# Cross-attention block with a quantised MLP: a split wait on TensorE, another form for five VectorE copies, and one step moved in VectorE's order

## The reference, cut to what matters

```python
# B=32 batches, T=100 tokens, D=256, S=361 context rows, H=16 heads of DK=64
Qh = einsum('btd,hdk->bhtk', layernorm(x), WQ)
Kh = einsum('btd,hdk->bhtk', ctx, WK)
Vh = einsum('btd,hdv->bhtv', ctx, WV)
attn = softmax(Qh @ Kh.T / sqrt(dk) + mask * -1e9)
x = x + concat_heads(attn @ Vh) @ WO
x = x + qlinear(gelu(qlinear(layernorm(x), W1, b1)), W2, b2)   # 8-bit codes, scales over the whole tensor
```

## Time and profile before

| what | value |
|---|---|
| median of 3 runs | 1129.66 us (1129.05 to 1130.61) |
| the profiled execution | 1126.18 us |
| its span, first to last instruction | 1124.1 us |
| TensorE busy | 1018.1 us, 91% of the span |
| VectorE busy | 978.2 us, 87% |
| ScalarE busy | 865.1 us, 77% |
| GpSimd busy | 770.6 us, 69% |
| the VectorE copies of L946 | 160, 131.5 us in all |

### The profile page before, as it was taken

How to read it: one execution, slowest core, us unless ns; L and a number is a source line. 1 busy time by engine, 2 the same in 40 slices (tenths; PEclk the granted TensorE clock), 3 DMA queues, 4 the chain that set the end, 5 groups by cost and what they waited for, 6 DMA issues and landing times.

```text
span 1124.1 us, 37431 instructions
## 1 busy us (share of the span) xinstructions
PE 1018.1 (91%) x10489; PEld 643.3 (57%) x10489; DVE 978.2 (87%) x2528; ACT 865.1 (77%) x1805; POOL 770.6 (69%) x1108
## 2 busy tenths in 40 slices
PE   3999999999999999999999999999999999985808
PEld 2555566666666666666666666666666666653307
DVE  5777999999999999999999999999999999973997
ACT  4555888888888888888888888888888888873916
POOL 2246877777777777777777777777777777773700
PEclk9999999999999999999999999999999999996969
DMA  8301665555555555555555555555555555555003
GB/s 253 113 1 31 130 134 131 131 135 135 135 135 131 130 135 132 130 131 134 135 135 135 135 135 135 132 130 130 134 135 135 132 130 130 134 132 153 1 0 117
DMA packets 441419, 138.22 MB, mean 123 GB/s; under 512 B 413650, under 2 KB 440374, under 8 KB 441398
## 3 DMA queue, kind: packets, MB, share of 16 engines
q1 hardware_dynamic: 441398, 137.96, 51.0%
HBM read 28.60 MB, written 6.55 MB: 31 GB/s over the span
## 4 chain that ended last, share of the span: by engine, by line
PE 75%; DVE 10%; ACT 5%; issue 4%; POOL 3%; DMA 1%; DVEq 1%; ACTq 0%; SPq 0%; POOLq 0%
PE front L341 19%; PE front L343 17%; PE front L342 17%; PE back L1226 8%; PE front L1208 6%; PE tp L1208 5%; POOL hl L585 3%; DVE hrange L1059 2%; DVE hrange L1060 2%; DVE prob L939 2%; ACT prob L711 2%; DVE k_l L959 1%; ACT q_h L749 1%; PE front L1291 1%; ACT ctx_h L745 1%
## 5 line engine op out<-in xcount | busy, mean ns | idle before, releaser
L585 POOL TENSOR_TENSOR hl<-prob,hl 100x361 f16<-100x361 f32 x512 | 432.1, 853 | 97.2 <-DVE hl L946 50.9
L711 ACT ACTIVATE prob<-prob,nmax 100x361 f32<-100x361 f32 x512 | 293.9, 587 | 47.7 <-DVE nmax L939 47.5
L341 PE MATMUL front<-ctx_h,wk_h 128*128 128x362 f16 x512 | 164.2, 321 | 31.3 <-POOL ctx_l L574 17.8
L1226 PEld LDWEIGHTS back<-v,pT 128*128 128x128 f16 (+1 forms) x4608 | 165.1, 98 | 45.1 <-issue 9.6
L717 ACT ACTIVATE hl<-prob 100x361 f16<-100x361 f32 x352 | 176.0, 500 | 7.9
L1226 PE MATMUL back<-v,pT 128*128 128x65 f16 (+1 forms) x4608 | 174.2, 194 | 6.3 <-DMA pT<-hl 6.2
L343 PE MATMUL front<-ctx_h,wk_l 128*128 128x362 f16 x512 | 161.7, 316 | 0.0
L342 PE MATMUL front<-ctx_l,wk_h 128*128 128x362 f16 x512 | 161.5, 315 | 0.0
L721 ACT ACTIVATE k_h<-front 128x362 f16<-128x362 f32 x256 | 118.9, 464 | 54.7 <-PE front L343 54.7
L959 DVE SCALAR_TENSOR_TENSOR k_l<-front,k_h 128x362 f16<-128x362 f32 x256 | 135.2, 528 | 24.4 <-ACT k_h L721 21.8
L939 DVE CUSTOM_DVE_ANT_0 prob<-front,mask_g,ngain 100x361 f32<-100x361 f32 x256 | 149.6, 584 | 2.2
(11 more groups left out here) (180 smaller groups left out, 1980.8 us busy)
## 6 DMA issues: line engine op xcount, KB each, us to landing
ctx_raw<-ctxT SPq DMA_DIRECT2D x33, 361.0 KB, 3.1
pT<-hl SPq DMA_TRANSPOSE x256, 3.1
xs<-x SPq DMA_DIRECT2D x8, 400.0 KB
q_all<-x SPq DMA_DIRECT2D x32, 100.0 KB
out<-q_all SPq DMA_DIRECT2D x32, 100.0 KB
xb<-out SPq DMA_DIRECT2D x5, 640.0 KB, 7.5
out<-xb SPq DMA_DIRECT2D x25, 128.0 KB, 1.8
q_all<-wq SPq DMA_DIRECT2D x1, 1024.0 KB, 6.6
```

The lines of the kernel that those rows point to most:

```text
L341: eng.matmul(dst, lh, rh, start=first, stop=False)
L585: pool.tensor_tensor(hl[0:T, n % RT, 1, 0:S], prob[0:T, n % RP, 0:S], hl[0:T, n % RT, 0, 0:S], ALU.subtract).then_inc(s_lo, 1)
L711: act.activation(prob[0:T, n % RP, 0:S], prob[0:T, n % RP, 0:S], ACT.Exp, bias=nmax[0:T, n:n + 1], scale=-1.0).then_inc(s_exp, 1)
L1226: ins = pe.matmul(obank[j % 2][:, n % GH * DV:(n % GH + 1) * DV], pT[0:r, n % RT, part_ * ST + st, :], v2[half][0:r, st, v, n % HT, :], st ...
```

## The change

Three edits. The wait of K0 for both pieces of `ctx_l` becomes a wait for the first piece ahead of the first three matmuls and for the second ahead of the other three. The five VectorE copies of a high half of the probabilities in each turn become a multiply by one and add of zero that also writes out a sum, into a new tile `hsum` that nothing reads. The due time of MAX14 becomes 10.619 in place of 9.245, which moves it from the last place of a turn to the place behind K0's low half, that is, `k_l` of K0 goes ahead of MAX14.

```diff
     MAX=(-2.253, -1.786, -0.98, -0.598, 0.248, 0.373, 0.602, 1.062, 3.199, 3.682, 5.123, 7.009, 7.8, 8.323,
-        9.245, 12.252),
+        10.619, 12.252),
...
+    hsum = place("hsum", [P, 1], F32)
...
                     wait(dve, s_exp, H * a + h + 1)
                     wait(dve, s_pv, H * a + h // 2 * 2 + 1 - RT)
-                    dve.tensor_copy(hl[0:T, h % RT, 0, 0:S], prob[0:T, h % RP, 0:S]).then_inc(s_hv, 1)
+                    dve.tensor_scalar(hl[0:T, h % RT, 0, 0:S], prob[0:T, h % RP, 0:S], 1.0, 0.0, ALU.mult, ALU.add,
+                                      accum_out=hsum[0:T, 0:1]).then_inc(s_hv, 1)
...
                 if kind == "K":
-                    if n == 0:
-                        wait(pe, s_c, KD * (a + 1))
                     ms = slice(n * P, (n + 1) * P)
                     for k in range(KD):
+                        if n == 0:
+                            wait(pe, s_c, KD * a + k + 1)
                         ins = split3(pe, ps[:, 0:SE], (wk_h[:, k, ms], wk_l[:, k, ms]),
```

## The result

The changed kernel takes 1121.7 us in the median of 5 runs, against 1129.66 us for the kernel before; the ratio is 0.9934, 95% interval 0.9921 to 0.9947. It is faster by 8.0 us. The forecast was 14.0 us: the direction came out, and so did the wait that sets the turn (K3's, for K1's `k_l`). The size did not, since one step on VectorE was far slower than forecast.

A forecast was written before the change was run, and what follows sets the result against it. TensorE's late starts at a turn's beginning, waiting for `ctx_l` and `k_l`, bound the kernel. They fall from 1.46 to 1.00 us, gaining 0.45 in each of 31 turns, 14.0 us: 1115.7 us forecast, range 1108.5 to 1124.

The forecast's parts named there:

- What bounds the kernel: At a turn's start TensorE waits for `ctx_l` (17.8 us in all) and VectorE's `k_l` (12.3 us); K3's start sets the gain.
- the anchor: TensorE's 521.00, when both `ctx_l` pieces are ready; set by a chain from the last V product that no edit shortens.
- Edit 1: On TensorE, K0's issue ends 0.46 us earlier a turn, with a 0.23 us wait for the second `ctx_l` piece.
- Edit 2: On VectorE, the pass takes 0.52 us and its read 0.08, mostly hidden; head 11's copy ends at 521.6, not 522.89.
- rival 2: GpSimd also holds the copies' new form on VectorE: K3 0.08 us later a turn, 1132.2 us; chance 0.07.
- The failing step: On VectorE at a turn's start, LN4 takes 0.07 us start to start behind head 11's copy, freeing VectorE near 521.7.
- Edit 3: VectorE idles from 521.7 to 522.43 before K0's `k_l`; K2 starts 0.96 us earlier, K3 0.45 us earlier.
- rival 3: Late `k_h` lengthens VectorE's idle time, or a dearer copy takes 0.2 us: gain 0.1 to 0.3 a turn, 1120 to 1126.5; chance 0.11.
- Past K3 all is covered: Later in the turn VectorE is at least as far ahead as TensorE; work queued behind MAX14 comes 0.3 to 0.6 us earlier.
- The signs named beforehand: Passes near 0.52 us, K3 waiting some 0.6, VectorE idling about 0.7; TensorE's `k_l` waits about 20 us, `ctx_l` under 8.

The follow-up runs named there:

- the extra subtraction: Changed kernel plus one unused 361-column GpSimd subtraction, behind LO10 (1113.35 us) or, in a second kernel, ahead of it (1113.77 us).
- The kernels bound at V1: Changed kernel with NORM1 moved behind K1's low half, 1116.25 us; the same without the step LN4, 1110.71 us.

## Why the prediction was right in direction and off in size

- **What bounds the kernel**: right. The start of `ctx_l` is the anchor, and TensorE's last late start behind it, K3's, sets the turn: as long as NORM1 kept its place a turn stayed at 23.36 us plus K1's low half, whatever became of K0 and K2.
- **Edit 1**: right in the mechanism. Three matmuls run ahead of the second piece, whose wait was 0.23 in the forecast and 0.77 - 0.46 = 0.31 by the starts (519.05, 519.82). K0 alone does not make the turn; undone by itself the edit costs 3.0 us.
- **Edit 2**: its own price was right, 0.52 and 0.08 forecast, 0.525 and 0.083 measured, no spread, and the read hidden (next start 0.44 behind). GpSimd does not hold this form, so rival 2 fell. The Trainium skill (SBUF — State Buffer, "Who interferes with whom") excepts the form that also writes out its accumulator from those that contend with GpSimd. The trace agrees: 160 passes between 0.521 and 0.536 us.
- **The failing step** is the one that has VectorE free at about 521.7 with "LN4 behind the copy, 0.07 from start to start". I took that 0.07 from a place where GpSimd had just stopped, and moved it to a place where it had not. LN4 measured 1.17 us, 1.09 from start to start. The same section of the Trainium skill says that a VectorE instruction with two SBUF inputs contends with a GpSimd instruction that reads SBUF; LN4 has two, and I had applied the section to the copies alone. That made K0's low half 521.44 + 1.18 = 522.62, not 522.43, and everything behind it 0.19 later. 31 x 0.19 = 6 us is the difference of 14.0 and 8.0. By the table the turn itself is 0.23 shorter, 31 x 0.23 = 7.1 us; the last microsecond of the 8.0 is not placed.
- **Edit 3**: I had written that VectorE would idle ahead of K0's low half where MAX14 could have stood. That idle time did not come, because LN4 filled it. So the edit neither cost nor gained, 1121.7 against 1121.93. It showed its cost only without LN4.
- **The range and the rivals**: 1121.7 lies in the band of rival 3, "a smaller gain", but neither of its reasons was the cause: `k_h` did not come late (it ended at 521.19, and K0's low half waited for LN4), and no other copy cost TensorE a wait. No rival named a small operation held by GpSimd. That the time fell inside the range is in part luck.
- **Past K3 all is covered**: right, by a small margin. The kernels bound at V1 have turns of 20.01 and 20.02 us plus K3's low half; in the changed kernel that sum would be 8.11 + 20.01 = 28.12, against the 28.31 that K3 sets. V1's wait appears when NORM1 is put between K1's and K3's low halves, and not at some time of K1's low half.
- **The signs named beforehand**: the copies, K0's parts, K2 and K3's late start came as written (K3 0.66 behind TensorE's own readiness, 522.95 to 523.61). TensorE's waits for `k_l` came to 15.3 us and not 20, as the list counts 0.50 of each 0.66. VectorE's idle time of 0.7 us was absent, and that absence was the mark of the failed step.

## What to carry to other kernels

When a long operation is shortened or moved, look at the GpSimd timeline under each operation that slides into the freed stretch, down to the smallest: a two-column compare was held for a microsecond. Read what an edit is worth from the one operation that the late start waits for (here K1's low half), not from the first wait that it takes away: edits 1 and 3 without edit 2 made K0's low half 4.11 - 3.59 = 0.52 us earlier and the turn not at all. And after each gain look for the next late operand before adding gains up.

## What the runs showed of the hardware

- A two-column VectorE operation with both inputs in SBUF, 0.15 us long with GpSimd idle, took 1.17 us when it came during GpSimd's work. It was released at the end of a GpSimd operation, not when GpSimd stopped: LN4 ended within 0.02 us of the end of Q0, of the extra subtraction or of LO10, whichever stood fourth in the stretch. The 1.80 us copy of the earlier trace rows, which began during LO10, ended 0.22 behind Q0 in the same way.
- It was not always the second operation from its arrival: LN4 that came during Q0 took 0.16 us with the next operation right behind Q0, and LN4 that came once during the first of five took 0.59 us and ended with that first one. What decides is not shown.
- One more GpSimd operation in that stretch made the kernel faster (turn 28.14 against 28.31 us): the operation at whose end LN4 was released was 0.14 us shorter (0.81 against 0.95) or, with LO10 there, 0.07.
- A pass that also writes out a sum, over 361 float32 columns in SBUF, took 0.521 to 0.536 us in 160 passes beside GpSimd's work, where the plain copy took 0.34 to 1.86.
